# A transformer and state-space block on one core: an opening order of its own for the first batch, and four residual tiles

## The reference, cut to what matters

```
h  = layernorm(x) * (1 + ca) + sa
xn = layernorm(h) * ln1_w + ln1_b
q, k, v = xn @ q_w + q_b, xn @ k_w + k_b, xn @ v_w + v_b          # 16 heads of 16
attn_out = softmax(causal(q k^T / 4)) v @ o_w + o_b
x_ssm, z = split(xn @ in_proj_w)                                  # 512 channels each
x_c  = silu(causal_conv4(x_ssm) + conv_b)
x_dbc = x_c @ x_proj_w                                            # 16 for dt, 16 for B, 16 for C
dt   = softplus(x_dbc[:16] @ dt_w + dt_b)
h_t  = exp(dt * A) * h_(t-1) + (x_c * dt) * B_t ;  y_t = C_t h_t  # 512 channels x 16 states
ssm_out = ((y + x_c * D) * silu(z)) @ ssm_out_w
x1 = h + alpha * attn_out + (1 - alpha) * ssm_out
x2 = x + ga * (x1 + gelu(layernorm(x1) @ w1 + b1) @ w2 + b2)
out = x2 + gb * (h3 @ base_w^T + base_b + 2 * top2_experts(h3)),  h3 = layernorm(x2) * (1 + cb) + sb
```

## Time and profile before

| what | value |
|---|---|
| time, median of 3 runs | 5196.59 us (5196.34 to 5197.73) |
| profiled execution, its own time | 5201.05 us |
| its span | 5199.2 us |
| mean granted clock of TensorE | 0.989 |
| PE busy | 4974.5 us, 96% |
| DVE busy | 4751.3 us, 91% |
| POOL busy | 4629.3 us, 89% |
| ACT busy | 4016.0 us, 77% |
| chain that ended last, by engine | PE 71%, DVE 10%, issue 8%, POOL 6%, DMA 2% |
| TensorE's granted clock in the first of 40 slices | 0.7 |

### The profile page before, as it was taken

How to read it: one execution, slowest core, us unless ns; L and a number is a source line. 1 busy time by engine, 2 the same in 40 slices (tenths; PEclk the granted TensorE clock), 3 DMA queues, 4 the chain that set the end, 5 groups by cost and what they waited for, 6 DMA issues and landing times.

```text
span 5199.2 us, 94534 instructions
## 1 busy us (share of the span) xinstructions
PE 4974.5 (96%) x32280; PEld 3447.1 (66%) x32280; DVE 4751.3 (91%) x7332; ACT 4016.0 (77%) x6403; POOL 4629.3 (89%) x2925
## 2 busy tenths in 40 slices
PE   5899999999999999999999999999999999999997
PEld 2567666667666667666677667677666676666665
DVE  4999999999999999999999999999999999999984
ACT  4777887877887877877877878878878778878773
POOL 4899999999999999999999999999999999999983
PEclk7999999999999999999999999999999999999998
DMA  5555555554555554555555555545555555555541
GB/s 150 159 152 154 158 166 160 163 156 154 163 161 164 159 163 148 164 167 158 160 153 159 167 167 160 156 152 159 170 161 158 155 155 162 160 164 159 161 141 55
DMA packets 522016, 812.29 MB, mean 156 GB/s; under 512 B 80976, under 2 KB 227832, under 8 KB 521536
## 3 DMA queue, kind: packets, MB, share of 16 engines
q1 hardware_dynamic: 516768, 805.96, 51.2%
q10 hardware_dynamic: 4768, 0.28, 0.1%
HBM read 716.57 MB, written 88.38 MB: 155 GB/s over the span
## 4 chain that ended last, share of the span: by engine, by line
PE 71%; DVE 10%; issue 8%; POOL 6%; DMA 2%; ACT 1%; SPq 1%; DVEq 0%; POOLq 0%; ACTq 0%
PE pY L984 12%; PE pM L1133 9%; PE pM L1145 8%; PE pM L1026 4%; PE pM L1120 4%; PE pM L1060 4%; DVE pD L1262 4%; PE pM L1073 4%; PE pM L993 4%; PE pM L1006 3%; POOL state L600 3%; PE pM L1093 3%; PE pM L1034 2%; PE pM L1117 2%; PE pM L1041 2%
## 5 line engine op out<-in xcount | busy, mean ns | idle before, releaser
L600 POOL TENSOR_TENSOR state<-scan_in,bc 128x1024 f32<-128x1024 f32 x1024 | 2406.7, 2363 | 145.4 <-PE pY L984 136.5
L745 ACT ACTIVATE pD<-scan_in,A 128x512 f32<-128x512 f32 x2048 | 1404.4, 690 | 401.5 <-DVE state L1270 315.9
L1262 DVE TENSOR_TENSOR_SCAN pD<-pD,state 128x512 f32<-128x512 f32 x1280 | 1545.2, 1219 | 69.0 <-ACT pD L745 67.7
L984 PE MATMUL pY<-ident,state 128*128 128x128 f32 x8192 | 1153.2, 275 | 32.4 <-POOL state L588 25.0
L588 POOL TENSOR_TENSOR state<-state,bc 128x512 f32<-128x512 f32 x768 | 969.6, 1274 | 155.8 <-DVE state L1262 155.8
L984 PEld LDWEIGHTS pY<-ident,state 128*128 128x128 f32 x8192 | 907.9, 142 | 267.8 <-issue 108.7
L1301 DVE TENSOR_REDUCE mx<-pM 128x1 f32<-128x512 f32 (+3 forms) x1408 | 860.1, 630 | 154.7 <-PE pM L1075 146.7
L1262 DVE TENSOR_TENSOR_SCAN state<-pD,state 128x512 f32<-128x512 f32 x768 | 916.4, 1210 | 57.7 <-ACT pD L745 57.6
L846 ACT ACTIVATE region<-pM 128x512 f32<-128x512 f32 (+1 forms) x1408 | 741.7, 559 | 177.8 <-PE pM L1095 153.9
L1270 DVE TENSOR_TENSOR state<-pD,bc 128x512 f32<-128x512 f32 x1280 | 862.1, 680 | 11.0
L1073 PE MATMUL pM<-region 96*128 96x512 bf16 (+3 forms) x2048 | 521.4, 301 | 24.8 <-DVE region L1318 12.1
(11 more groups left out here) (172 smaller groups left out, 8068.1 us busy)
## 6 DMA issues: line engine op xcount, KB each, us to landing
bc<-bc_d SPq DMA_DIRECT2D x2048, 256.0 KB, 3.9
region<-qk_d SPq DMA_DIRECT2D x640, 128.0 KB, 3.7
qk_d<-qkp SPq DMA_DIRECT2D x64, 384.0 KB, 3.4
qk_d<-ht SPq DMA_DIRECT2D x64, 384.0 KB, 5.1
xt<-in_x_dram SPq DMA_DIRECT2D x32, 512.0 KB, 5.4
hres_d<-xt SPq DMA_DIRECT2D x32, 512.0 KB, 4.4
region<-qk_d SPq DMA_DIRECT2D x256, 64.0 KB, 3.1
x<-hres_d SPq DMA_DIRECT2D x32, 512.0 KB, 5.2
```

What stands on the lines that cost most here:

```text
L600: nc.gpsimd.tensor_tensor(state[:, at_:at_ + JP], us[:, parity(b), k // N * JP:(k // N + 1) * JP, :], bc[:, k % BC_SLOTS, 0, :].unsqueeze( ...
L745: act.activation(pD[DECAY_BANK[e]][:], dts[:, parity(b), j], ACT.Exp, scale=A[:, j, n:n + 1]).then_inc(a_ok.sem, 1)
L984: ins = pe.matmul(y_part(t, e % JP), state[:, e % RING, t * P:(t + 1) * P], ident[:], is_transpose=True, start=False, stop=(e % PASS >= PA ...
L1262: v.tensor_tensor_scan(h if e in POOL_C else decay, decay, h, 0.0, ALU.mult, ALU.add)\
```

## The change

`drive` now takes a second list per engine, EARLY. The steps that it names are run for batch 0 first, in its order. What is left of the opening and of the first turn follows in the order of before. From the second turn on nothing moves. In the lists, the convolution's four blocks stand ahead of the pieces of q and k, and x projection, dt and softplus ahead of the last piece, qk3. GpSimd has `u0 fill0` ahead of that piece's two steps, and SyncE the first four row loads ahead of its write.

For batch 0 the four float32 copies and residuals of q and k go into four tiles (`residual_of`, in a part of `region` that is not in use yet) in place of the one tile that is shared with `dbc`. So ScalarE's copy of piece n no longer waits for the low part of piece n - 1, nor does the copy xp wait for the last low part. Two waits are added: the first row load waits for `bc_out`, and TensorE's xs0 waits for `xt_ok`.

```diff
@@ -354,21 +355,28 @@
-        def drive(eng, order, step, banks=()):
+        def drive(eng, order, step, early, banks=()):
...
-            for name, shift in order:
-                if shift > 0:
-                    step(name, Batch(None, 0))
-            for n in range(B):
-                turn(Batch(None, n), n == 0, n == B - 1)
+            opening = [(name, 0) for name, shift in order if shift > 0]
+            opening += [(name, shift) for name, shift in order if shift >= 0]
+            for name in early:
+                opening.remove((name, 0))
+            for name, n in [(name, 0) for name in early] + opening:
+                step(name, Batch(None, n))
+            for n in range(1, B):
+                turn(Batch(None, n), False, n == B - 1)
...
+        def residual_of(b, n):
+
+            return qk_first[:, n] if b.off == 0 else qkf[:]
...
+                if b.off == 0 and k == 0 and row == 0:
+                    b.wait(sp, bc_out)
...
-                    nc.gpsimd.tensor_tensor(qkf[:], qkf[:], qk_parts[n % 2][:, 0], ALU.subtract).then_inc(qk_r.sem, 1)
+                    nc.gpsimd.tensor_tensor(residual_of(b, n), residual_of(b, n), qk_parts[n % 2][:, 0], ALU.subtract).then_inc(qk_r.sem, 1)
...
-                    if n:
+                    if n and b.off:
                         b.wait(act, qk_lo, n)
-                    else:
+                    elif b.off:
                         b.wait_last(act, dt_ps)
                         b.wait_last(act, bc_out)
...
-                    b.wait(act, qk_lo)
+                    if b.off:
+                        b.wait(act, qk_lo)
...
+                    if j == 0 and b.off == 0:
+                        b.wait(pe, xt_ok)
...
+EARLY = {engine: text.split() for engine, text in {
+    "SP": "load qk0 qk1 xp qk2 rb0 rc0 rb1 rc1 qk3 ld0 l1a",
+    "POOL": "l0s l0a l0b l0c l1s qr0 ql0 qr1 ql1 qr2 ql2 u0 fill0 qr3 ql3 fill1 u1",
+    "ACT": "l0a l1a xt0 xt1 xs0 xs1 xs2 xs3 qk0 xsilu qm0 qk1 qm1 qk2 xp dt0 dt1 qm2 dt2 dt3 sp2 qk3 qm3",
+    "PE": "xt0 xt1 xs0 xs1 xs2 xs3 qk0 qk1 qk2 xp dt0 dt1 dt2 dt3 qk3",
+    "DVE": "l0s l1s xs0 xs1 xs2 xs3",
+}.items()}
```

More of the change, by code:

```diff
@@ L231, in adaln_block @@
         shared = at[0]
+        qk_first = region[:, shared:shared + 4 * L].rearrange("p (n t) -> p n t", n=4)
         oT = view(L)
@@ L530, in step @@
                     sp.dma_start(out[b.index].rearrange("(t p) f -> p t f", p=P), nrm(b)).then_inc(out_done.sem, 16)
-            drive(sp, ORDER["SP"], step)
+            drive(sp, ORDER["SP"], step, EARLY["SP"])
             sp.wait_ge(out_done.sem, 16 * B)
@@ L633, in step @@
                     b.wait(pool, qk_mid, n + 1)
-                    nc.gpsimd.tensor_tensor(qk_parts[n % 2][:, 2], qkf[:], qk_parts[n % 2][:, 1], ALU.subtract)\
+                    nc.gpsimd.tensor_tensor(qk_parts[n % 2][:, 2], residual_of(b, n), qk_parts[n % 2][:, 1], ALU.subtract)\
                       .then_inc(qk_lo.sem, 1)
@@ L680, in _ @@
             pool.wait_ge(built, BUILT)
-            drive(pool, ORDER["POOL"], step)
+            drive(pool, ORDER["POOL"], step, EARLY["POOL"])
         @block.scalar
@@ L784, in step @@
                                    bias=qkv_b[:, n // 2, n % 2:n % 2 + 1]).then_inc(qk_hi.sem, 1)
-                    if n:
+                    if n and b.off:
                         b.wait(act, qk_lo, n)
-                    else:
+                    elif b.off:
                         b.wait_last(act, dt_ps)
                         b.wait_last(act, bc_out)
-                    act.activation(qkf[:], pM[bank_of(name)][:], ACT.Identity,
+                    act.activation(residual_of(b, n), pM[bank_of(name)][:], ACT.Identity,
                                    bias=qkv_b[:, n // 2, n % 2:n % 2 + 1]).then_inc(qk_f.sem, 1)
@@ L794, in step @@
                     b.wait(act, qk_r, n + 1)
-                    act.activation(qk_parts[n % 2][:, 1], qkf[:], ACT.Copy).then_inc(qk_mid.sem, 1)
+                    act.activation(qk_parts[n % 2][:, 1], residual_of(b, n), ACT.Copy).then_inc(qk_mid.sem, 1)
                 elif name[0] == "v":
@@ L911, in step @@
                     act.activation(axT(b), pM[bank_of(name)][:], ACT.Copy).then_inc(axt_ok.sem, 1)
-            drive(act, ORDER["ACT"], step)
+            drive(act, ORDER["ACT"], step, EARLY["ACT"])
         @block.tensor
@@ L1177, in step @@
                     ins.then_inc(out_ps.sem, 1)
-            drive(pe, ORDER["PE"], step, banks)
+            drive(pe, ORDER["PE"], step, EARLY["PE"], banks)
         @block.vector
@@ L1400, in step @@
                         ins.then_inc(o_fin.sem, 1)
-            drive(dve, ORDER["DVE"], step)
+            drive(dve, ORDER["DVE"], step, EARLY["DVE"])
 MAX_FILLS = ([(3, [h]) for h in range(G)] + [(2, [h]) for h in range(G)]
```

## The result

| | before | with the change |
|---|---|---|
| time, median (lowest to highest) of 14 runs | 5198.33 us (5193.67 to 5205.29) | 5208.76 us (5203.86 to 5215.41) |
| profiled execution, its own time | 5201.05 us | 5210.25 us |
| its span | 5199.2 us | 5208.4 us |
| mean granted clock of TensorE | 0.989 | 0.987 |
| PE / DVE / POOL / ACT busy, us | 4974.5 / 4751.3 / 4629.3 / 4016.0 | 4972.0 / 4752.4 / 4629.5 / 4017.3 |

The ratio of the times is 1.0020 (95% interval 1.0012 to 1.0028): the kernel became 10.4 us slower by the medians and 9.2 us by the two profiled executions. The median of before is 1.7 us above the one of three runs that stood ahead of the prediction. No engine's work changed by more than 2.5 us, so what was lost is waiting.

A forecast was written before the change was run, and what follows sets the result against it. The first turn starts at VectorE's pace, its start set by two paths meeting at scan0. The walk gave 9.9 us later, taken as 9.7: 5196.59 + 9.7 = 5206.3 us, range 5200.5 to 5209.5.

The forecast's parts named there:

- the sum: Whole kernel: profiled execution of before, 5201.05 us, plus 9.7 us gives 5210.75, standing for a median of 5206.3.
- the rival with half clock through dt: Opening, dt on TensorE: every dt group takes twice as long, 2.7 us more, 12.4 slower, 5209.0 us; chance 0.20.
- step 2: Opening, x projection: copy xp ends at 75.1, 7.2 us won, with qk2's copies waiting for qk0's write.
- step 3: Opening, dt and softplus: done at 83.45 against 89.96, 6.5 us won, with 0.75 us added for one slow group.
- step 4: Opening, fill0, last q/k piece, its write, ld0, scores, reductions: scan0 at 106.05 against 96.14, 9.9 us later.
- The two paths: Opening: x projection's path and the q/k reductions meet at scan0; shortening one alone gives 0.36 us at most.
- the walk: Opening: sum over five steps with durations of the profile's rows, ending with scan0 9.9 us later.
- The write's landing: Opening, q/k writes through HBM: 3.3 us each; 8.4 us shift in all with the page's 2.0 for one write.
- From the first score to scan0: Opening, first score to end of the fourth reduction: 6.05 us, as before, scan0 starting at once.
- step 5: After scan0: GpSimd's lead of 5.4 us costed at nothing, so the opening's shift is handed on rigidly.
- GpSimd's lead counts: First turn: GpSimd sets the pace, its 5.4 us lead is paid back, 4.3 us slower, 5200.9 us; chance 0.12.
- x projection's path alone counts: Opening: scan0 follows fill0's end at 87.15, 8.9 us earlier, 5187.7 us; chance 0.05.

The follow-up runs named there:

- repeated run: The changed kernel measured once more, nothing altered, on the same chip as e5 and e6; 5209.89 us against 5201.54 of before, ratio 1.0016.
- e5: The changed kernel with row loads rb2 and rb3 ahead of qk3's write and ld0 on SyncE; 5212.08 us against 5201.54 of before, ratio 1.0021.
- e6: The changed kernel with qr3 and ql3 ahead of fill0 on GpSimd; 5208.30 us against 5201.54 of before, ratio 1.0014.
- e1: The changed kernel with convolution and q/k pieces interleaved, all four pieces ahead of x projection, ld0 right behind xp; 5198.08 us against 5202.00 of before, ratio 0.9994.
- e3: The changed kernel with all EARLY lists empty: four residual tiles, order of before; 5200.74 us against 5202.00 of before, ratio 0.9995.
- e7: e1's lists with u1 ahead of fill1 on GpSimd; 5197.89 us against 5201.04 of before, ratio 0.9991.
- e8: e7's lists with the values' groups v0 and v1 moved into the holes of the convolution; 5195.21 us against 5201.04 of before, ratio 0.9991.
- e4: The changed kernel with the values' groups v0 and v1 ahead of the first scores; 5209.47 us against 5202.00 of before, ratio 1.0013.

## Why the prediction was right

The forecast was 9.7 us later than before; measured were 9.2 by the profiled executions (5210.25 against the 5210.75 of the sum) and 10.4 by the medians. The repeated run is 8.35 us above before by the medians, so these leave about 2 us open. Put as a time, the forecast was 5206.3 us; the median, 5208.76, is 2.5 us above it, of which 1.7 are the higher median of before. It lies next to the 5209.0 of the rival with half clock through dt, and only the traces tell the two apart. Point by point, with the traced times as they stand and the difference of 0.8 us in the start of the opening in the second column:

| step | predicted end | measured | plus 0.8 |
|---|---|---|---|
| copy xp (step 2) | 75.1 | 73.32 | 74.1 |
| copy of dt3 (step 3) | 80.15 | 78.64 | 79.5 |
| softplus whole (step 3) | 83.45 | 81.95 | 82.8 |
| fill0 (step 4) | 87.15 | 85.85 | 86.7 |
| ql3 (step 4) | 90.15 | 88.85 | 89.7 |
| first read of ld0 (step 4) | 93.45 | 91.47 | 92.3 |
| first score (step 4) | 100.0 | 98.00 | 98.8 |
| scan0 (step 4) | 106.05 | 104.52 | 105.3 |

**The two paths** held. The chain of waits after goes through the steps of the walk from softplus on, in its order. The convolution and x projection came out as walked, with the slow group that was taken for dt3: two short matmuls took 2.07 us at 75.84, where six had taken 1.98 just before. ScalarE's copy of qk2 did wait for the write of qk0, 0.82 us (ScalarE's row at 71.56).

**The write's landing** was mis-sized. Step 4 took 3.3 us, the median of one buffer in the earlier trace rows; the chain of waits has 2.52. The same holds for qk0's write in step 2, which was issued at 68.95 and had landed by 71.56. The 3.3 is the median of two writes of unlike kind, by the landing times of each in the kernel before: the one issued at 55.97 landed in 2.5 us, the one at 73.65 in 4.0, having gone out 0.40 us behind the write of `ht`. The two of `ht` took 2.6 each, and after the change all four took 2.5 to 2.8. So the 2.6 of the other buffer was the right row for qk3's write, which has none just ahead of it, and with it the walk's 9.9 becomes 9.2. The estimate by the page's 2.0 us, 8.4 us in all, was further off: the Trainium skill, "DMA: Bandwidth & Descriptors", "Rules for kernel authors", gave the direction, the trace the size.

**From the first score to scan0** was mis-sized the other way. Step 4 took 6.05 us "as before"; it was 6.52 (98.00 to 104.52). TensorE in the kernel before (timeline):

```profile
90.77 3.41 PE L1034 MATMUL pM<-w_qkv,xnT 128*128 128x256 f32 x8
94.02 0.38 PE L1073 MATMUL pM<-region 96*128 96x512 bf16 x1
```

There the values' eight matmuls took 3.41 us, and the scores behind them ran at full clock, 0.38 us; after, 3.73, and the next score took 0.63. That the clock came back later because TensorE had idled 16.38 us ahead of the scores, against 3.81 in the earlier trace rows, is likely. The four traces with 14 to 16.5 us of idle time there (the change, its repeat, e5, e6) have 3.73 us for these eight matmuls and 0.61 to 0.63 for the next score; the four with 3.7 to 4.1 us (before, e1, e3, e7) have 3.13 to 3.60 and 0.38. No run changed the idle time alone. So from the `xnT` mark ql3 ended 0.5 us ahead of the walk, its write landed 0.7 sooner, and the scores gave 0.5 back: the 0.7 us between the walk's 9.9 and the measured 9.2. That two of these cancel is luck.

**The shift is rigid** (step 5) held within 1 us: 8.4 us at scan0, 8.35 at the next layer norm, 9.2 at the end. (The 9.2 at scan0 is counted from the `xnT` mark and is another measurement than this one; that they are equal is chance.) GpSimd waited for VectorE 1.90 us at 116.84, as it had 1.89 at 108.47.

**The rivals.** That GpSimd's lead counts fell with e5. That x projection's path alone counts fell with the first trace: softplus was 8.0 us earlier (7.2 from the `xnT` mark) and the scan 8.4 later. The half clock through dt did not happen in full in any trace. In the repeated one, whose opening starts where that of before does, dt3's copy ended at 80.83; the sum had 80.15, the rival 82.9. The prediction treated the clock as one of two worlds; it is a matter of degree and of the execution, and dt's eight matmuls took 4.5 to 5.2 us over the five traces with the change's order. The medians average over that; whether it is why they differ from the profiles was not shown.

Not tried was the change's order with the one shared tile: the copy xp would overwrite the residual of qk2 before GpSimd's two steps on it are done. So the tiles' worth within the new order is open. Open too is why e1, e7 and e8, with VectorE 6 to 7 us ahead at the first layer norm, keep only 4 to 6 of them at its last row. The variants of the change differ there by as much (e4 has 8.1 us at the layer norm and 5.7 at the end), so that one profile of each can't tell a real give-back from scatter.

## What to carry to other kernels

When the chain of waits names one path, look at the rows just ahead of the join on the waiting engine: a second path may end within half a microsecond (here 0.36 us), and then shortening the named one is worth that gap and no more. Before moving a step back to let another pass, follow the whole of what it feeds; here two steps of GpSimd (4.7 us) and three copies behind softplus put 9 us on a path with two trips through HBM, while e1 got x projection just as early without paying at all. And a loss ahead of a saturated engine's first piece of work wasn't won back by a lead elsewhere (7.7 us of GpSimd's, in e5): in both traces of the change it is there at the end, within 1 us. What a gain ahead of it is worth is less sure, since e1, e7 and e8 kept 4 to 6 us of 6 to 7.

## What was not expected of the hardware

The same program's opening took 60.17 us in one execution and 61.63 in another, because the clock was at its lower level (granted 0.50, which is 1.2 GHz) in other parts of the convolution and dt: the same eight matmuls took 5.16 us in the first and 6.44 in the second. Comparisons of openings to a microsecond need the clock's rows beside them, or several executions. And the clock fell within dt: TensorE had idled 2.23 us, six short matmuls of 16 rows took 1.98 us, and the two behind them, after 0.50 us more of idle time, 2.07; the granted clock is 1.00 until 75, 0.91 from 75 to 76 and 0.50 after. The Trainium skill, "TensorE: Matmul & The Clock Gate", Part 1, says that the monitor behind the clock runs on its own and doesn't start over with a kernel. The variation between executions agrees with that; no run here shows what makes it lower the clock.
